# Two places for the split attended rows, and the output projection moved up to fill every batch of a period

## The reference

```python
q = (x @ wq_w.T + wq_b).reshape(b, t, H, HD)      # H = 32, HD = 32
k, v = (one head each)
scores = einsum('bqhd,bkd->bhqk', q, k1) / sqrt(HD)
scores = where(causal, scores, -inf)
attn = einsum('bhqk,bkd->bqhd', softmax(scores), v1).reshape(b, t, H * HD)
y = attn @ wo_w.T + wo_b
x1 = layernorm(x + y)
x_sim, w_sim = clip(x1 * x_scale), clip(weight * w_scale)   # scales 448 / max|.|
out = layernorm(x1 + x_sim @ w_sim / (x_scale * w_scale))
```

## Time and profile before

| what | value |
|---|---|
| median of 3 runs | 2524.83 us (2523.31 to 2526.2) |
| the profiled execution | 2527.55 us |
| its span, first to last instruction | 2525.8 us |
| attention stage, with the batches counted here | from 453 to about 2104 us |
| batches of the stage | 272 |

### The profile page before, as it was taken

The page is one execution under the profiler, slowest core; times in us unless marked ns, Lnnn a source line. Parts: engine busy times, 40 slices in busy tenths (PEclk is TensorE's granted clock), DMA queues, the critical chain, the costliest instruction groups (busy, mean ns, idle before and its releaser), DMA issues.

```text
span 2525.8 us, 36171 instructions
## 1 busy us (share of the span) xinstructions
PE 2410.3 (95%) x14312; PEld 1559.5 (62%) x14312; DVE 1747.1 (69%) x1293; ACT 1300.9 (52%) x1412; POOL 803.3 (32%) x442
## 2 busy tenths in 40 slices
PE   6999999799999999999999999999999993999998
PEld 5888887245555555555555555555555553888887
DVE  6334335798888887888888878888888773444444
ACT  2222223677777777777777777777777652000000
POOL 2232221112323322332232223322332322566653
PEclk9999999899999999999999999999999996999999
DMA  7434433432221122122222221222121203222221
GB/s 231 144 116 142 149 130 116 106 105 63 60 64 43 44 63 64 43 61 46 64 43 45 62 64 43 51 56 64 43 64 43 51 34 117 83 83 91 91 85 65
DMA packets 150742, 198.01 MB, mean 78 GB/s; under 512 B 8558, under 2 KB 108878, under 8 KB 148558
## 3 DMA queue, kind: packets, MB, share of 16 engines
q1 hardware_dynamic: 126990, 144.71, 22.0%
q10 hardware_dynamic: 23616, 51.39, 5.3%
HBM read 123.72 MB, written 72.35 MB: 78 GB/s over the span
## 4 chain that ended last, share of the span: by engine, by line
PE 81%; DVE 7%; ACT 5%; issue 3%; POOL 2%; DMA 1%; SPq 0%; ACTq 0%; DVEq 0%; POOLq 0%
PE bank L1152 17%; PE bank L1164 15%; PE bank L1049 15%; PE bank L1223 14%; PE bank L1137 13%; DVE acc L936 5%; ACT prob L704 4%; PE bank L1174 2%; PE bank L1182 2%; POOL att_lo L580 1%; PE bank L1212 1%; ACT att_hi L718 1%; PE bank L1134 1%; DMA xt_raw<-x_t 1%; PE bank L1035 1%
## 5 line engine op out<-in xcount | busy, mean ns | idle before, releaser
L704 ACT ACTIVATE prob<-bank 128x1024 f32<-128x1024 f32 x1088 | 1055.3, 1022 | 439.3 <-PE bank L1152 431.8
L936 DVE TENSOR_TENSOR acc<-acc,prob 128x2048 f32<-128x2048 f32 x420 | 987.5, 2351 | 105.2 <-ACT prob L704 87.1
L1152 PE MATMUL bank<-q_st,keys 98*128 98x512 f32 x2176 | 645.0, 416 | 32.2 <-ACT prob L704 22.1
L1152 PEld LDWEIGHTS bank<-q_st,keys 98*128 98x128 f32 x2176 | 376.9, 189 | 367.5 <-ACT prob L704 263.3
L1164 PE MATMUL bank<-prob,v_t 128*32 128x512 f32 x4352 | 528.4, 604 | 0.0
L575 POOL TENSOR_SCALAR_AFFINE_SELECT prob<-prob 128x1024 f32<-128x1024 f32 x128 | 183.0, 1453 | 734.7 <-ACT prob L704 734.6
L1164 PEld LDWEIGHTS bank<-prob,v_t 128*32 128x32 f32 x4352 | 114.2, 109 | 265.0 <-issue 253.7
L932 DVE TENSOR_TENSOR acc<-prob 128x2048 f32<-128x2048 f32 x60 | 137.5, 2292 | 155.8 <-ACT prob L704 142.5
L1049 PE MATMUL bank<-xt_hi,w_hi 128*128 128x512 f32 x576 | 228.2, 396 | 16.8 <-DVE xt_lo L778 16.1
L1049 PE MATMUL bank<-xt_hi,w_lo 128*128 128x512 f32 x576 | 227.2, 394 | 0.0
L1049 PE MATMUL bank<-xt_lo,w_hi 128*128 128x512 f32 x576 | 226.8, 394 | 0.0
(11 more groups left out here) (109 smaller groups left out, 2553.5 us busy)
## 6 DMA issues: line engine op xcount, KB each, us to landing
q_st<-q_hi_d SPq DMA_DIRECT2D x128, 256.0 KB
xt_raw<-x_t SPq DMA_DIRECT2D x16, 1024.0 KB, 7.0
q_hi_d<-part_hi ACTq DMA_DIRECT2D x64, 256.0 KB, 2.1
q_lo_d<-part_lo ACTq DMA_DIRECT2D x64, 256.0 KB, 2.3
q_st<-q_lo_d SPq DMA_DIRECT2D x64, 256.0 KB
res<-x SPq DMA_DIRECT2D x32, 512.0 KB, 5.9
x_d<-res SPq DMA_DIRECT2D x32, 512.0 KB, 2.7
x<-x_d SPq DMA_DIRECT2D x32, 512.0 KB, 3.2
```

What stands on the lines that cost most here:

```text
L704: nc.scalar.activation(prob[:, s % SLOTS, 2 * p:2 * p + 2], bank[:, 2 * p:2 * p + 2], ACT.Exp, scale=SCALE).then_inc(p_done, 1)
L936: nc.vector.tensor_tensor(acc[:, n % 2], acc[:, n % 2], new, ALU.add).then_inc(acc_done, 1)
L1152: last = nc.tensor.matmul(bank[:, g].rearrange("p (a n) -> p a n", n=P), keys[:, k // QT, k % QT * P:(k % QT + 1) * P], queries[:, :, g], ...
```

## The change

There are two places for att_hi and att_lo, used in turn (q % 2), so ACT waits only for the projection of the tile before the last one. Room for them comes from `piece`, the staging place for the last stage's weights, which now is the second half of `res`. Tile 1's residual load waits until the pieces are sent. The residual load is issued at the step HALF0 (`row_at`), where it was issued at SPLIT. In every period the second tile's SPLIT goes from step 21 to 13 (17 to 11 in period 15), its HALF0 from batches 12 to 15 to batches 11 to 14, and its HALF1 from four batches, 16 to 19, to five, 15 to 19. In period 15 the halves go from batches 10 to 12 and 13 to 15 to batches 9 to 11 and 12 to 15. Its SUM0 comes two steps earlier, and SUM1, DEVIATION, SCALE_ROW and LARGEST stay.

```diff
-            piece = sb("piece", [P, D], F32, s)
-            q_st2 = sb("q_st2", [SM, 2 * HG, 2 * P], F32R, s)
...
-            s.enter_context(nc.sbuf_tensor("wo_stage_rest", [P, 2 * D - 2 * P], F32))
+            s.enter_context(nc.sbuf_tensor("w_lo_rest", [P, D - 2 * P], F32))
+            att_hi0 = sb("att_hi0", [P, KT, P], F32R, s)
+            att_lo0 = sb("att_lo0", [P, KT, P], F32R, s)
+            q_st2 = sb("q_st2", [SM, 2 * HG, 2 * P], F32R, s)
...
-            att_hi = sb("att_hi", [P, KT, P], F32R, s)
-            att_lo = sb("att_lo", [P, KT, P], F32R, s)
+            att_hi1 = sb("att_hi1", [P, KT, P], F32R, s)
+            att_lo1 = sb("att_lo1", [P, KT, P], F32R, s)
             res = sb("res", [P, 2, D], F32, s)
+            piece = res[:, 1]
+            att_hi, att_lo = (att_hi0, att_hi1), (att_lo0, att_lo1)
...
-                names = (21, 24, 30, 30, 32, 38, 38, 39, 44, 45) if second else (4, 6, 12, 12, 14, 20, 20, 22, 27, 28)
+                names = (13, 22, 28, 28, 30, 38, 38, 39, 44, 45) if second else (4, 6, 12, 12, 14, 20, 20, 22, 27, 28)
...
-                names = (17, 20, 24, 24, 26, 30, 30, 31, 34, 35) if second else (4, 6, 10, 10, 12, 16, 16, 18, 22, 23)
+                names = (11, 18, 22, 22, 24, 30, 30, 31, 34, 35) if second else (4, 6, 10, 10, 12, 16, 16, 18, 22, 23)
...
-                if s in split_at:
-                    q = split_at[s]
+                if s in row_at:
+                    q = row_at[s]
                     if q >= 2:
                         sp.wait_ge(x1_sent[q % 2], 16 * (q // 2))
                         sp.wait_ge(measured, q - 1)
+                    if q == 1:
+                        sp.wait_ge(piece_sent, 16 * KT)
...
-            pool.wait_ge(wo_cut, KT)
+            pool.wait_ge(qkv_done, (TB + 2) * MT)
             nc.gpsimd.memset(share[:].bitcast(F32), 2.0 / P).then_inc(fixed, 1)
...
-                    nc.gpsimd.tensor_tensor(att_lo[:], att[:, q % TILES_KEPT], att_hi[:].bitcast(F32), ALU.subtract).then_inc(att_cut, 1)
+                    nc.gpsimd.tensor_tensor(att_lo[q % 2][:], att[:, q % TILES_KEPT], att_hi[q % 2][:].bitcast(F32), ALU.subtract).then_inc(att_cut, 1)
...
-                    act.wait_ge(y_done, 2 * q)
-                    nc.scalar.activation(att_hi[:], att[:, q % TILES_KEPT], ACT.Copy).then_inc(att_hi_cut, 1)
+                    act.wait_ge(y_done, max(2 * q - 2, 0))
+                    nc.scalar.activation(att_hi[q % 2][:], att[:, q % TILES_KEPT], ACT.Copy).then_inc(att_hi_cut, 1)
...
-                    last = nc.tensor.matmul(dst, (att_hi, att_lo)[a][:, k], (wo_hi, wo_lo)[c][:, k, cols],
+                    last = nc.tensor.matmul(dst, (att_hi, att_lo)[a][q % 2][:, k], (wo_hi, wo_lo)[c][:, k, cols],
```

More of the change, by code:

```diff
@@ L314, in build @@
                     fillers.setdefault(place, []).append((q, half, place - first // 2, (last - first) // 2 + 1))
+        row_at = {places(q)[HALF0]: q for q in range(TILES)}
         PIECE_EVERY, PIECE_CLIP = 6, 4
@@ L383, in _ @@
             sp.wait_ge(qkv_done, (TB + 1) * MT + 1)
-            sp.dma_start(piece[:], b_o).then_inc(bo_in, 16)
+            sp.dma_start(piece, b_o).then_inc(bo_in, 16)
             q_hi_h = q_hi_d.rearrange("t (h p) n -> t p h n", p=HD)
@@ L461, in _ @@
                             sp.wait_ge(piece_sent, 16 * k)
-                        sp.dma_start(piece[:], w_f[:, k]).then_inc(piece_in, 16)
+                        sp.dma_start(piece, w_f[:, k]).then_inc(piece_in, 16)
                     if place == PIECE_CLIP + 1:
                         sp.wait_ge(piece_clip, 2 * k + 2)
-                        sp.dma_start(wf_sim_d[:, k], piece[:]).then_inc(piece_sent, 16)
-                if s in split_at:
-                    q = split_at[s]
+                        sp.dma_start(wf_sim_d[:, k], piece).then_inc(piece_sent, 16)
+                if s in row_at:
+                    q = row_at[s]
                     if q >= 2:
@@ L695, in _ @@
             act.wait_ge(bo_in, 16)
-            nc.scalar.activation(bo_parts[:], piece[:], ACT.Copy).then_inc(bo_cut, 1)
+            nc.scalar.activation(bo_parts[:], piece, ACT.Copy).then_inc(bo_cut, 1)
             for s in range(STEPS + SLOTS_OVER):
@@ L917, in _ @@
             dve.wait_ge(bo_cut, 1)
-            nc.vector.tensor_tensor(bo_parts[P // 2:P], piece[P // 2:P], bo_parts[P // 2:P].bitcast(F32), ALU.subtract).then_inc(bo_cut, 1)
+            nc.vector.tensor_tensor(bo_parts[P // 2:P], res[P // 2:P, 1], bo_parts[P // 2:P].bitcast(F32), ALU.subtract).then_inc(bo_cut, 1)
             for s in range(STEPS + SLOTS_OVER):
@@ L943, in _ @@
                     dve.wait_ge(piece_in, 16 * (k + 1))
-                    nc.vector.tensor_scalar(piece[:], piece[:], small[:, 15:16], FP8_MAX, ALU.mult, ALU.min).then_inc(piece_clip, 1)
+                    nc.vector.tensor_scalar(piece, piece, small[:, 15:16], FP8_MAX, ALU.mult, ALU.min).then_inc(piece_clip, 1)
                     dve.wait_ge(piece_clip, 2 * k + 1)
-                    nc.vector.tensor_scalar(piece[:], piece[:], -FP8_MAX, None, ALU.max).then_inc(piece_clip, 1)
+                    nc.vector.tensor_scalar(piece, piece, -FP8_MAX, None, ALU.max).then_inc(piece_clip, 1)
                 if s in sum0_at:
```

## The result

The changed kernel takes 2511.5 us (median of 5 runs, 2509.48 to 2516.22) against 2524.83 before: a ratio of 0.9946, 95% interval 0.9935 to 0.9957, or 13 us less. I had forecast 2499.6 and a range from 2494 to 2511. The direction and the place were right. Half of the gain is missing, and the time lies just outside the range.

A forecast was written before the change was run, and what follows sets the result against it. Each attention-stage batch was taken to cost the larger of a 5.36 us ring and PE's work. The terms summed to -25.2 us, taking the 2524.83 us median to 2499.6; range 2494 to 2511.

The forecast's parts named there:

- (b) to (g): Batches 11, 12, 15, 16, 17 to 19 and period 15, in turn: +7.1, -4.7, -1.7, -9.3, -8.0, -1.3 us.
- The ring: Attention stage: scores, two exponential steps on ACT, last scores and weighing hold a batch at 5.36 us.
- the clock: Clock falls in batches 6.11 and 15.9, without filler, go once filled: -3.3 us, bounds 0 and -3.3.
- (a): Batch 3: with two places ACT cuts att_hi earlier and PE's wait for att_lo goes, 11 x 0.49 = -5.4 us.
- (f): Batches 17 to 19: five fillers for six save 0.23 us in 35 of 42, -8.0 us.
- (h): Second tile's att_hi and att_lo at step 13, not 21: held-up DVE sums cost +1.4 us in periods 1 and 9.
- DVE passes on part of its lateness: Batch 11 waits for DVE's late add, giving back 7 to 12 us: 2507 to 2512; chance 0.15.
- PE is full: Matmul work bounds the stage, so only waits go: -9 to -14 us, 2511 to 2516; chance 0.08.

The follow-up runs named there:

- experiment 3: Changed kernel with the old steps for SPLIT and the halves, keeping only the two places for att_hi and att_lo: 2527.4 us, ratio 1.0004 to the kernel before.
- experiment 5: Kernel before, one place and old steps, with att_lo cut in two instructions that PE waits for separately: 2516.78 us, ratio 0.9954 to the kernel before.
- experiment 6: Changed kernel with att_lo cut in two instructions that PE waits for separately: 2503.41 us, ratio 0.9911 to the kernel before.
- experiment 4: Changed kernel with the second tile's SPLIT at step 17 for 13: 2508.15 us, ratio 0.9929 to the kernel before.
- experiment 1: Changed kernel with ACT's old wait before att_hi given back for the first tile of each period: 2514.63 us, ratio 0.9957 to the kernel before.
- experiment 7: Changed kernel with att_lo in two parts and the second tile's SPLIT at step 17: 2498.51 us, ratio 0.9889 to the kernel before.
- experiment 2: Changed kernel with att_lo filled by a one-input GpSimd copy, the subtraction left out: 2497.23 us, ratio 0.9887 to the kernel before.

## Why the prediction was right and wrong

**Right: what bounds the stage, and (b) to (g).** The ring of 5.36 us under batches with up to six fillers, and 0.23 us for each matmul above it, gave six terms that sum to -17.9 and measured -17.9. PE's busy share, 95% before and 96% after, tells nothing of it. The spreads that the ring had hidden in batch 11 came out at +1.06, and in 8.12, 1.16, 2.16 and 10.16 the waits for DVE went. Batch 9.16 kept 0.3 of its.

**Right: the clock.** Among the ten profiles, the three kernels with an empty batch 11 (before, experiments 3 and 5) all have the fall in batch 6.11, and before and experiment 5 the one in 15.9. None of the seven with it filled has either. Two falls came in filled batches, both with a long wait of PE: experiment 6 in 1.7 (2.14 us) and experiment 5 in 8.12 (1.94 us). Experiment 4 has one in 15.16, which has no filler in any of the kernels. In period 0, unfilled in all, it comes and goes.

**Wrong: (a), the wait for att_lo.** The failed step is "Before, ACT could cut att_hi at step 4 only when PE had finished batch 2. Then POOL wrote att_lo and PE waited". I took the chain of waits (PE's filler, att_hi, att_lo, bias) for the cause. It was one of two chains of nearly equal length: in period 4 of the kernel before it had att_lo issued 0.40 us before the sum ended. The other, exponentials, sum, att_lo, ended last, and it hadn't changed. Removing ACT's wait moved att_lo's issue by 0.9 us and its end by nothing (experiments 1 and 3). Two parts moved what PE waits for, and gave the 5.4 without any second place (experiment 5).

**Wrong: a saving counted ahead of a wait.** (f) takes 0.23 us off batch 19, and eleven times the next batch waits for something that hangs on ACT and DVE. That is +2.6 in (a)'s row. I had said that plain batches on the ring give nothing back, and had not applied it to a batch that waits. With the wait gone, experiments 6 and 7 have it back: 0.72 a batch, not 0.49.

**Too small: (h).** The rule of the Trainium skill that spoke against the change (GPSIMD Engine Reference, Specifications) names the mechanism that took the missing gain, and I had its row. I priced only one direction, the sum held up by att_lo, and only in periods 1 and 9. Of the 2.5 us that (h) lacks, half lie there, where the second sum also ran into GpSimd's masking (experiment 4). The other half lie in batch 8 of periods 3 and 11 (+0.45 each) and batch 9 of 6 and 14 (+0.2 each), where I had said that 2 us or more were left. The other direction, att_lo held up by the sum, was at step 4 all the time; the 12 us that experiments 2 and 7 win are its price and that of step 13. The rule's condition is on VectorE's instruction alone, two SBUF inputs as the sum has, and these runs agree: GpSimd's one-input copy was held up too (2.21 us for 1.03). My expectation of experiment 2 had put the condition on GpSimd's side.

**Two rivals had the time and not the place.** *DVE passes on part of its lateness* gave 2507 to 2512, but batch 11 never waited for the add. *PE is full* gave 2511 to 2516, but a bias and six fillers went into a plain batch 11 for 0.15 us, and fillers were worth 0.23 us a matmul where they left. That 2511.5 lies in both ranges speaks for neither.

Why the medians differ by 13.3 us and the profiles by 16.0 isn't shown; the profiled execution of before had three clock falls of 1.6 us in the stage, and the other executions have no trace.

## What to carry to other kernels

Sort batches by their content and compare lengths, not busy shares: an empty slot as long as a full one is room, and its size can be forecast to tenths of a us. Before a wait is removed, look for what else ends at the same time as the awaited instruction: if its duration changes with its start and its end does not, suspect that it waits inside, for something that no semaphore shows. Here GpSimd's work with a deadline gained by being cut in pieces, with the first piece alone in front of the consumer, and by a place where no VectorE sum with a deadline stood behind it.

## What the runs showed of the hardware

While a VectorE sum of two SBUF tensors ran (2.29 us), a GpSimd instruction issued in it had its time counted from the sum's end: 2.26 us for a subtraction of 128x1024 (2.35 alone), 0.90 for a copy (1.03 alone). A sum issued in the subtraction ended 2.14 us after it. This holds beyond the rows shown. In the six profiles with att_lo in one piece as a subtraction, 100 were issued inside a sum, at least 0.3 us before its end, and all ended 2.23 to 2.27 us after it; 114 sums began inside one, and all ended 2.14 to 2.16 us after it. Whichever had begun first kept the other out until its end. Not all of VectorE's work is held up: 73 adds of a bank to `res` (L915), with one of their two inputs in PSUM, began inside an att_lo and took their usual 0.63 to 0.69 us. The clipping, with one input and that in SBUF, was held up (1.64 us for 0.69, experiment 6). In none of these rows does the profile show a wait for the other engine. The held instruction is listed as busy, which is why GpSimd's busy time rose by 19 us with the same work.
